# Attention and mixture-of-experts layer: tiles 0 to 13 list their tokens per expert in DRAM and compute the experts in jobs of 128 rows after the attention

## The reference

```
x = x + xattn(layernorm(x), ctx, itok, ...)
xn = layernorm(x)
gate_logits = xn @ gate_w + gate_b                     # [tokens, 8]
_, top_idx = top_k(gate_logits, 2)
all_out = relu(einsum('nsd,edo->nseo', xn, expert_w) + expert_b)   # 8 experts, 256 -> 256
x = x + take_along_axis(all_out, top_idx[..., None], axis=2).mean(axis=2)
```

## Time and profile before

| | us |
|---|---|
| time, median of 2 runs (450.34 to 450.71) | 450.52 |
| the profiled execution, its own time | 450.26 |
| its span, first to last instruction | 448.4 |

### The profile page before, as it was taken

The page is one execution under the profiler, slowest core; times in us unless marked ns, Lnnn a source line. Parts: engine busy times, 40 slices in busy tenths (PEclk is TensorE's granted clock), DMA queues, the critical chain, the costliest instruction groups (busy, mean ns, idle before and its releaser), DMA issues.

```text
span 448.4 us, 9783 instructions
## 1 busy us (share of the span) xinstructions
PE 422.8 (94%) x2574; PEld 317.6 (71%) x2574; DVE 260.5 (58%) x1153; ACT 288.2 (64%) x940; POOL 265.8 (59%) x363
## 2 busy tenths in 40 slices
PE   2967999999999999999999999999999999999995
PEld 2836676777777777777777777777777777777663
DVE  2657757565656565655656565656565565656341
ACT  1225676776676767676767667676767676766633
POOL 4034556576565657574757656575757475765555
PEclk9968999999999999999999999999999999999998
DMA  9990000000000000000000000000000000000001
GB/s 214 273 376 36 2 1 2 1 1 2 12 2 14 1 15 0 12 0 12 0 12 0 0 12 0 12 0 12 0 12 0 12 0 13 1 1 13 0 12 31
DMA packets 16529, 12.54 MB, mean 28 GB/s; under 512 B 7568, under 2 KB 16128, under 8 KB 16240
## 3 DMA queue, kind: packets, MB, share of 16 engines
q1 hardware_dynamic: 13488, 10.64, 8.1%
q10 hardware_dynamic: 2880, 1.43, 1.4%
q0 software_dynamic: 128, 0.09, 0.1%
HBM read 10.04 MB, written 2.10 MB: 27 GB/s over the span
## 4 chain that ended last, share of the span: by engine, by line
PE 81%; POOL 4%; issue 3%; DVE 3%; ACT 2%; DVEq 0%; POOLq 0%; ACTq 0%
PE psum L544 18%; PE psum L545 12%; PE psum L546 12%; PE psum L875 11%; PE psum L961 8%; PE psum L913 7%; PE psum L885 6%; PE psum L943 4%; ACT prob L1006 1%; POOL q_sb L1045 1%; DVE xn L471 1%; POOL acc L1074 1%; POOL acc L1071 1%; PE psum L440 1%; PE psum L552 1%
## 5 line engine op out<-in xcount | busy, mean ns | idle before, releaser
L1097 POOL TENSOR_TENSOR prob<-prob,prec 128x512 f32<-128x512 f32 x64 | 68.4, 1069 | 83.5 <-DVE prec L1231 83.5
L1006 ACT ACTIVATE prob<-nsc,nmax 128x128 f32<-128x128 f32 x256 | 99.7, 395 | 0.0
L1045 POOL TENSOR_TENSOR q_sb<-rope_a,rope_b 128x256 f32<-128x256 f32 x64 | 47.0, 734 | 57.8 <-DVE rope_b L1160 57.7
L875 PEld LDWEIGHTS psum<-kT_all,qT 128*128 128x128 f32 x512 | 68.0, 193 | 6.0 <-issue 0.4
L875 PE MATMUL psum<-kT_all,qT 128*128 (+1 forms) x512 | 68.4, 277 | 0.0
L1176 DVE CUSTOM_DVE_ANT_0 nsc<-psum,mask 128x128 f32<-128x128 f32 x256 | 59.2, 286 | 14.9 <-PE psum L875 14.9
L1027 ACT ACTIVATE eout<-psum,gates 128x256 f32<-128x256 f32 x128 | 54.0, 476 | 19.9 <-DVE gates L1240 10.4
L994 ACT COPY qT<-psum 128x512 f32<-128x512 f32 x64 | 37.5, 586 | 43.6 <-PE psum L913 43.6
L544 PE MATMUL psum<-we_hi,xT_hi 128*128 128x512 f32 x128 | 57.3, 448 | 0.0
L1231 DVE RECIPROCAL prec<-psum_h 128x4 f32<-128x4 f32 x64 | 11.4, 178 | 74.6 <-ACT prob L1006 74.6
L546 PE MATMUL psum<-we_hi,xT_lo 128*128 128x512 f32 x128 | 50.4, 394 | 0.0
(11 more groups left out here) (131 smaller groups left out, 863.2 us busy)
## 6 DMA issues: line engine op xcount, KB each, us to landing
wo_raw<-in_w_o SPq DMA_DIRECT2D x2, 1024.0 KB, 10.7
we_raw<-in_expert_w SPq DMA_DIRECT2D x1, 2048.0 KB, 14.4
out<-acc SPq DMA_DIRECT2D x16, 128.0 KB, 1.7
x_all<-in_x SPq DMA_DIRECT2D x2, 640.0 KB, 7.9
ctxT<-in_ctx_t SPq DMA_DIRECT2D x2, 512.0 KB, 7.2
wuqT<-in_w_uq_t ACTq DMA_DIRECT2D x1, 768.0 KB, 13.4
wukT<-in_w_uk_t SPq DMA_DIRECT2D x1, 512.0 KB, 11.3
x_all<-in_x SPq DMA_DIRECT2D x1, 512.0 KB, 13.2
```

Of the source, the lines that this page charges most:

```text
L875: mm = pe.matmul(B_S[r][:, h, :], qT[r][:, h, :], keys, start=True, stop=True)
L1006: e = act.activation(prob[r][:, h, :], nsc[r][:, h, :], ACT.Exp, bias=nmax[r][:, h:h + 1], scale=-1.0, accum_out=psum_h[r][:, h:h + 1])
L1045: pool.tensor_tensor(q_sb[1 - r][:, :, KVC:P], rope_a[1 - r][:], rope_b[1 - r][:], ALU.add).then_inc(m["rope_joined"], 1)
L1097: pool.tensor_tensor(p[:], p[:], prec[r][:, :].unsqueeze(2).to_broadcast([P, HG, P]), ALU.mult).then_inc(m["prob_normed"], 1)
```

## The change

For tiles 0 to 13 the expert groups leave the slots; tiles 14 and 15 keep them, as 8 dense groups in the drain. The position of everything else in a slot stays. Instead:

- In `g` = 1 two small matmuls count, per expert, the rows that have chosen it before each row. In `g` = 2 DVE works out for each row its two places in the lists (eight small instructions behind the normed row), in `g` = 3 POOL sends the normed row with its token number twice to `slots` in DRAM with an indirect DMA. Each expert has a region of 1792 rows.
- In `prep`, SP also writes 128 padding rows to each of the 8 regions, and POOL sets constants.
- After the last group DVE computes a table of 35 jobs (28 blocks of rows and 7 for the blocks that are not full).
- After the walk each job: SP reads its first row from the table and loads 128 rows, PE transposes them and multiplies with one expert, whose column it also reads from the table (one bias matmul and six matmuls with 256 columns), ACT and DVE split the turned rows into two parts, ACT applies the relu with the scale 0.5, and POOL scatters the 128 results to `halves` in DRAM.
- When all 35 are there, SP loads `halves` (8 loads, 3.67 MB), DVE adds them to `x_all`, ACT stores the 14 tiles (4 stores, 1.84 MB).

The core of the diff (the same operations appear for the padding constants, the general path and the table, which is cut to its first and last lines):

```diff
 @prep.sync
+            sp.wait_ge(S("pad_set"), 2)
+            for e in range(NE):
+                sp.dma_start(slots.ap()[CAP * e:CAP * e + P, :], pad_row[:]).then_inc(S("padded"), 16)
...
 PE, slot
+                if g == 1 and live(t - 2, TILES) and gathered(t - 2):
+                    pe.matmul(B_E[:, 0:NE], before16[:], chosen16[:], start=True, stop=True)
+                    pe.matmul(B_E[:, NE:2 * NE], ones16[:], chosen16[:], start=True, stop=True).then_inc(m["rank_done"], 1)
                 f = i - 8
-                if live(f, GROUPS):
+                if dense_group(f):
...
 PE, after the walk
+            def job_turn(j):
+                pe.wait_ge(m[f"ld_job{j % 4}"], 16 * (j // 4 + 1))
+                at_least(pe, "jx_lo_done", j - 1)
+                for c in range(DC):
+                    mm = pe.transpose(JOB_TURNED[j % 2][:, P * c:P * c + P], wanted[j % 4][:, P * c:P * c + P], ident[:])
+                mm.then_inc(m["jT_done"], 1)
+            def jobs():
+                pe.wait_ge(m["table_done"], 1)
+                for j in range(NJ):
+                    if j == 0:
+                        job_turn(0)
+                    at = pe.value_load(job_cols[0:1, j:j + 1], min_val=0, max_val=O * (NE - 1))
+                    if j + 1 < NJ:
+                        job_turn(j + 1)
+                    pe.wait_ge(m["jx_lo_done"], j + 1)
+                    if j < 2:
+                        pe.wait_ge(m["relu_done"], GROUPS - GPT * NS)
+                    at_least(pe, "jrelu_done", j - 1)
...
 ACT, after the walk
+                    act.copy(jx_hi[j % 2][:], JOB_TURNED[j % 2][:, 0:D].rearrange("p (c n) -> p c n", c=DC)
+                             ).then_inc(m["jx_hi_done"], 1)
+                    if j > 0:
+                        job_relu(j - 1)
...
 POOL, slot
+                if g == 3 and live(t - 2, TILES) and gathered(t - 2):
...
+                    at_least(pool, "placed", t - 1)
+                    for high in range(2):
+                        pool.indirect_dma_start(slots.ap(), bass.IndirectOffsetOnAxis(place_i[j][:, high:high + 1], 0),
+                                                row[j][:], None, bounds_check=NE * CAP - 1, oob_is_err=False
+                                                ).then_inc(m[f"sent{j}"], 16)
 POOL, after the walk
+                for j in range(NJ):
+                    pool.wait_ge(m["jidx_done"], j + 1)
+                    pool.wait_ge(m["jrelu_done"], j + 1)
+                    pool.indirect_dma_start(halves.ap(), bass.IndirectOffsetOnAxis(jidx[j % 4][:, 0:1], 0), jout[j % 4][:], None,
+                                            bounds_check=2 * NS * P - 1, oob_is_err=False).then_inc(m[f"put{j % 4}"], 16)
...
 DVE, slot
                 if g == 0 and live(t - 2, TILES):
                     top_two("gate_step", t - 2, [5, 6])
-                    at_least(dve, "relu_done", GPT * (t - 3))
-                    dve.tensor_scalar(gates[j][:], gt2[:], 0.5, None, ALU.mult).then_inc(m["gates_ready"], 1)
+                    if gathered(t - 2):
+                        dve.tensor_copy(chosen16[:], gt2[:]).then_inc(m["chosen"], 1)
...
+                if g == 2 and live(t - 2, TILES) and gathered(t - 2):
+                    at_least(dve, "rank_done", t - 1)
+                    dve.tensor_tensor(place[:], B_E[:, 0:NE], filled[:], ALU.add).then_inc(m["place_step"], 1)
+                    dve.wait_ge(m["place_step"], n + 1)
+                    dve.tensor_tensor(taken[:], place[:], gt2[:], ALU.mult).then_inc(m["place_step"], 1)
+                    dve.wait_ge(m["place_step"], n + 2)
+                    dve.tensor_reduce(place_hi[:], taken[:], AX.X, ALU.max)
+                    dve.tensor_reduce(place_sum[:], taken[:], AX.X, ALU.add).then_inc(m["place_step"], 1)
+                    dve.wait_ge(m["place_step"], n + 3)
+                    dve.tensor_tensor(row[j][:, D + 1:ROW], place_sum[:], place_hi[:], ALU.subtract)
+                    dve.tensor_tensor(place_i[j][:, 0:1], place_sum[:], place_hi[:], ALU.subtract)
+                    dve.tensor_copy(place_i[j][:, 1:2], place_hi[:])
+                    dve.tensor_tensor(filled[:], B_E[:, NE:2 * NE], filled[:], ALU.add).then_inc(m["placed"], 1)
+                if isinstance(i, int) and i == GROUPS - 1:
+                    job_table()
...
 DVE, job_table (20 instructions) and jobs
+                dve.wait_ge(m["placed"], NS)
+                dve.tensor_tensor(counts[:], filled[:], region[:], ALU.subtract).then_inc(step, 1)
...
+                for j in range(NJ):
+                    dve.wait_ge(m[f"ld_job{j % 4}"], 16 * (j // 4 + 1))
+                    at_least(dve, f"put{j % 4}", 16 * (j // 4))
+                    dve.tensor_scalar(is_high[j % 4][:], wanted[j % 4][:, D + 1:ROW], job_region[:, j:j + 1], float(NS * P), ALU.is_lt,
+                                      ALU.mult).then_inc(m["is_high_done"], 1)
...
 SP, after the walk
+                for j in range(NJ):
+                    at = sp.value_load(job_row[0:1, j:j + 1], min_val=0, max_val=NE * CAP - P)
+                    at_least(sp, "jT_done", j - 3)
+                    at_least(sp, "jidx_done", j - 3)
+                    sp.dma_start(wanted[j % 4][:], slots.ap()[bass.ds(at, P), :]).then_inc(m[f"ld_job{j % 4}"], 16)
```

More of the change, by code:

```diff
@@ L104, in kernel_program @@
         seg_t = sb("seg_t", [P, 2])
-        x2 = [sb(f"x2_{i}", [P, D]) for i in range(2)]
         st2, mv2, veps2, rstd2 = sb("st2", [P, 6]), sb("mv2", [P, 2]), sb("veps2", [P, 1]), sb("rstd2", [P, 1])
-        x2n = sb("x2n", [P, D])
+        row = [sb(f"row{i}", [P, ROW]) for i in range(2)]
+        chosen16 = sb("chosen16", [P, NE], BF16)
+        place, taken = sb("place", [P, NE]), sb("taken", [P, NE])
+        place_hi, place_sum = sb("place_hi", [P, 1]), sb("place_sum", [P, 1])
+        place_i = [sb(f"place_i{i}", [P, 2], I32) for i in range(2)]
         xT_hi = [sb(f"xT_hi{i}", [P, DC, P], F32R) for i in range(2)]
@@ L414, in kernel_program @@
                  "wo_lo_done", "fold_o_mm", "we_hi_done", "we_lo_done", "qc_hi_done", "waits_passed",
-                 "rope_joined", "prob_normed", "rstd2_done", "acc_step", "out_stored0", "out_stored1"]
+                 "rope_joined", "prob_normed", "rstd2_done", "acc_step", "out_stored0", "out_stored1",
+                 "chosen", "rank_done", "place_step", "placed", "token_set", "sent0", "sent1", "table_step", "table_done",
+                 "ld_job0", "ld_job1", "ld_job2", "ld_job3", "jT_done", "jx_hi_done", "jx_lo_done", "jidx_done", "is_high_done",
+                 "je_done", "jrelu_done", "put0", "put1", "put2", "put3", "half_added", "sum_stored",
+                 *(f"ld_half{i}" for i in range(8))]
         m = {n: sem(n) for n in names}
+        shared = ("latent", "fold", "wo_", "we_", "x_", "waits", "logit", "out_stored", "sent", "ld_", "put", "sum_stored")
+        near_only = [n for n in names if not n.startswith(shared)]
+        m.update({n: m[near] for n, near in zip(general_names, near_only)})
         def at_least(eng, name, n):
@@ L527, in kernel_program, with gathered, dense_group, x2_of @@
         main = ctx.enter_context(nc.Block())
-        def expert_bank(f):
-            return B_Q if isinstance(f, int) and f > GROUPS - 8 and f % 2 else B_E
+        EXPERT_BANKS = [B_E, B_Q]
+        JOB_TURNED = [B_QT, B_PT]
+        SUM_PARTS = [slice(4 * n, min(4 * n + 4, NS)) for n in range(4)]
+        def gathered(tile):
+            return not isinstance(tile, int) or tile < NS
+        def dense_group(f):
+            return isinstance(f, int) and GPT * NS <= f < GROUPS
+        def x2_of(tile):
+            return x_all[:, bass.ds(tile, 1), :].rearrange("p a d -> p (a d)")
         def walk(eng, slot):
@@ L965, in _ @@
             near = pe.value_load(flag[0:1, 0:1], min_val=0, max_val=1)
+            def job_turn(j):
[16 more added lines that the diff above has]
+                    at_least(pe, "jrelu_done", j - 1)
+                    cols = bass.ds(at, O)
+                    z = EXPERT_BANKS[j % 2][:, 0:O]
+                    pe.matmul(z, ones3[:], bias3[:, cols], start=True, stop=False)
+                    for c in range(DC):
+                        mm = mm3(pe, z, jx_hi[j % 2][:, c, :], jx_lo[j % 2][:, c, :], we_hi[:, c, cols], we_lo[:, c, cols],
+                                 start=False, stop=(c == DC - 1))
+                    mm.then_inc(m["je_done"], 1)
             with pe.If(near == 1):
                 walk(pe, slot)
+                jobs()
             with pe.Else():
@@ L1260, in _ @@
             with sp.If(near == 1):
-                with sp.Fori(0, B) as b:
-                    for j in range(TPB):
-                        sp.wait_ge(m["acc_step"], 2 * GPT * (TPB * b + j) + 2 * GPT)
-                        sp.dma_start(out[bass.ds(TPB * b + j, 1)].rearrange("a p d -> p (a d)"),
-                                     acc[j][:]).then_inc(m[f"out_stored{j}"], 16)
```

(25 more changed lines are left out.)

203 lines of the change are left out of this document (163 added, 40 removed).

## The result

The changed kernel takes 551.6 us (median of 2, 550.37 to 552.83) against 450.52 before: a ratio of 1.224 (95% interval 1.219 to 1.229). The prediction was 543, range 500 to 590, slower. The profiled execution has a span of 548.6 us, 100.2 more than the 448.4 before.

What follows compares the result with a forecast made beforehand. It took a ring through ACT, POOL and PE once per slot, not PE's work, as the bound. 443.3 + 4.6 + 3.5 + 5.5 = 456.9, then + 2 + 63 + 3.4 + 18 = 543 us; range 500 to 590.

Steps and rivals of the forecast that it cites:

- Ring: In each slot: exponentials, norm, PE's transposes and ACT's copy in turn set 5.70 us; expert groups cost it nothing.
- g2 to g3: Slot step where DVE's place chain is added: `taken` held by POOL's norm, seven instructions behind; 7.4 us against 6.12.
- The walk as a whole: Slots of 14 tiles: two steps shorter by 0.43 and 0.45, g2 to g3 1.3 longer; +4.6 us.
- POOL: In g3, two indirect DMAs between join and norm, 1.2 us each, hidden in 3.3 us of room less 0.5.
- Start: End of `prep`: all engines wait for SP's eight more stores, 2.6 to 11 us, taken as +3.5.
- Table: 20 DVE instructions before slot 64's `oT_lo`, plus the norm's hold, delay the dense drain: +5.5 us.
- Jobs: After the walk: 35 jobs at PE's 1.8 us each, 0.6 of it a register load; 63 us.
- Tail: After the jobs: last relu, put and landing 3.4 us, then loads and stores at 376 GB/s, 18 us.
- PE as bound: Rival: PE's work sets the slots, about 4.2 us each; 105 us less, 434; chance 0.03.
- The hidden DVE chain: Rival: g2 to g3 at 5.7 and g0 to g1 at 5.4; 31 us less, 512; chance 0.14.
- Jobs at 1.3: Rival: register loads overlap with matmuls in the jobs; 17 us less, 526; chance 0.18.
- Indirect DMAs at 2.6: Rival: they set the jobs and delay g3; 56 us more, 599, the jobs alone 571; chance 0.18.

Runs made afterwards that it cites:

- four sends: The changed kernel with four indirect DMAs in g3 instead of two, the extra two to a spare DRAM list nobody reads: 586.7 us, ratio 1.302.
- place early: The changed kernel with the eight small place instructions and the cast chosen16 moved ahead of the reciprocal of their slots: 515.75 us, ratio 1.145.
- fixed column: The changed kernel with eight job buffers instead of four, and PE taking the expert's column from a constant instead of a register load: 549.5 us, ratio 1.220.
- no puts: The changed kernel without the puts of jobs 4 to 34, the tail reading x in place of halves: 543.9 us, ratio 1.204.

## Why the prediction was right, point by point

**Ring.** Right, and now shown: the slots without expert groups came out at the predicted 5.8, 6.1 and 5.4 (5.78, 6.03, 5.37), the version without any lists has all four (5.77, 6.03, 5.35, 5.71), and some 45 us of matmuls that nobody reads, in the same place, changed none. PE's 100% was the trap; the earlier trace rows showed the way out of it.

**g2 to g3.** Said 7.4, is 7.08. The hold was right (`taken` 0.81, predicted about 0.7, and 0.17 outside the norm). What was mis-sized are the instructions behind it: the prediction counted seven, there are six, and took them at 0.13 to 0.26 each, 1.17 in all, while from the end of `taken` (205.72) to `oT_lo` (206.30) are 0.58: five of the distances are 0.07 or 0.08. The other terms of the 7.4 were together 0.24 too low. With 7.08 in the sum the walk would have come out 13 x 0.3 = 4 us shorter, that is at about +0.6.

**The walk as a whole.** Said +4.6, is +9.8. The sum misses a term, PE's clock, and that it is only 5 off is luck: the pitch above erred the other way. In four tiles (norms at 161.17, 236.30, 311.42, 386.51) PE fell to 1.2 GHz for about 7 us; the fall begins some 4 us before these norms, inside the long step. Two steps took 7.50 and 7.67 in place of 7.08 and 5.77, 2.3 more per tile, 9.3 in all. The prediction's only use of a clock was to read 1.00 in the earlier trace rows; it did not ask what a PE with gaps would be granted.

**POOL.** The indirect DMA measured 0.97 to 1.15 us with 0.3 between two, 1.37 to 1.45 from one send to the next and 1.27 between the closest puts; said 1.2. Hidden in `g` = 3, right, but with 0.4 us to spare where the prediction reckoned 3.3 less 2.4 less 0.5, the same 0.4; four sends showed it.

**Start.** Said +3.5, is +3.6 in this execution and about 5 over all of them.

**Table.** DVE's `oT_lo` came at 440.83, 5.6 us behind the reciprocal where it was 0.95 before: 4.65, said 5.5. But PE had waited 4.01 us for it and then ran at 1.2 GHz at least until 447 (window above), and the stretch grew by 7.2. The prediction had only the wait, not what the wait does to the clock.

**Jobs.** Said 35 x 1.8 = 63, first relu to last is 58.35, 34 x 1.72. Right in size, partly by luck, since a load that was priced too high stood in for gaps that were not foreseen: the register load is 0.2 and not 0.6, PE's own pitch is 1.52 and not 1.8, and 0.2 come from gaps that belong to the puts. From the start of a put to the end of DVE's wait for it lie 2.5 to 3.4 us, mostly about 2.7; 481.07 to 484.51 above is the longest. The prediction's 1.2 + 1.7 = 2.9 for that was right. The Trainium skill (DMA: Bandwidth & Descriptors, "Latency and other measured facts") gives about 0.6 us as floor of a register load. What it costs beside running matmuls is the measured 0.2.

**Tail.** From the last relu to the tail's first load 3.46 (said 3.4), from there to the end 19.9 (said 18). The DMA moves 291 GB/s in that window, loads and stores together, not the 376 of the earlier trace rows.

**The total.** The parts of the prediction add up to a span of 543 and a time of 545, of which it said 543; measured are 548.6 and 551.6. The span is 5 us off: +5.2 in the walk, +1.7 in the dense drain, -1.6 behind it.

**Rivals.** PE as bound is excluded by the version without lists. The hidden DVE chain (512) is what "place early" made of it: 515.75 when the instructions really are out of the norm. Jobs at 1.3 would need both the fixed column and no puts, to go by the two runs; no version had both. Indirect DMAs at 2.6 were twice the truth.

## What to carry over

A busy share of 100% says who is busy, not who sets the pace: look for a stretch of the same trace that lacks the work to be removed, and read its step. Small instructions cost by their place, not by their size: eight of them and a cast behind a reciprocal, inside another engine's long instruction, cost 36 us over 14 tiles, and ahead of it nothing. Of the 36, 27 are the steps themselves and 9 are PE's clock. Work that leaves slots where it was hidden gives back little (1.9 us of PE in 56 slots was worth 15 us), and what replaces it in a stretch of its own is paid in full: lists, table, jobs and tail cost 116 (551.6 less 435.3).
